# A decoder layer with a gated delta rule branch and a mixture of experts: the delta rule's 128-wide blocks merged in four staggered groups, its exponentials moved to the middle of a head, the prologue worked in halves, and the first delta rule stage placed ahead of the experts

## The reference

```
xn = layernorm(x)
out = x + delta_branch(xn) + ffn_branch(xn)

delta_branch: qkvz = xn @ W_qkvz ; ba = xn @ W_ba        # 16 key heads, 2 value heads each
  q, k, v = silu(causal_conv4(q, k, v)) ; z = gate
  beta = sigmoid(b) ; g = -exp(A_log) * softplus(a + dt_bias) ; g = cumsum(g) in a chunk of 64
  decay = tril(exp(g_i - g_j)) ; M = -tril(k_beta k^T * decay, -1)
  T = (I - M)^-1                                        # solve_triangular, per chunk
  then a scan over chunks: o = (q e^g) S + (q k^T * decay) v' ; S = S e^g_last + k'^T v'
  out = (rmsnorm(o * silu(z)) * norm_weight) @ W_out

ffn_branch: x1 = rmsnorm(xn) ; causal attention, 16 heads of 128 ; hid = xn + attn
  x2 = rmsnorm(hid) ; top 4 of 16 experts (gated, width 176) + shared expert (width 352)
  return hid + routed + shared
```

## Time and profile before

| what | value |
|---|---|
| median of 3 runs | 1630.26 us (1629.26 to 1636.0) |
| profiled execution | 1629.19 us, its span 1627.4 us |
| PE busy | 1534.4 us, 94% of the span |
| DVE busy | 1111.6 us, 68% |
| ACT busy | 784.7 us, 48% |
| POOL busy | 438.4 us, 27% |
| steady head | about 59.2 us, 14 of them |

### The profile page before, as it was taken

One profiled execution on the slowest core, in us unless ns is written; L12 is line 12 of the kernel. 1 busy time (PEld: TensorE's weight loads), 2 busy tenths in 40 slices (PEclk: granted clock), 3 DMA queues, 4 the chain that ended last, 5 costly groups with the idle time before them and its releaser, 6 DMA issues.

```text
span 1627.4 us, 29153 instructions
## 1 busy us (share of the span) xinstructions
PE 1534.4 (94%) x10922; PEld 1081.3 (66%) x10922; DVE 1111.6 (68%) x2442; ACT 784.7 (48%) x1692; POOL 438.4 (27%) x277
## 2 busy tenths in 40 slices
PE   4999999999978995699999999999999999999987
PEld 3666666766656773376677677667668668667756
DVE  4544445465362333769889889988988988888875
ACT  3444345343413433445646645646555565564641
POOL 0000000003031005226335344444532531532410
PEclk8999999999998997889999999999999999999999
DMA  3234333223323323323234144143233223323201
GB/s 97 82 116 143 131 115 104 62 70 117 87 99 108 107 85 119 90 63 82 60 99 91 46 103 103 42 100 98 60 72 82 64 65 84 69 57 88 59 11 33
DMA packets 225051, 136.88 MB, mean 84 GB/s; under 512 B 160976, under 2 KB 196304, under 8 KB 224912
## 3 DMA queue, kind: packets, MB, share of 16 engines
q1 hardware_dynamic: 221840, 126.62, 28.6%
q0 software_dynamic: 3072, 8.39, 1.6%
HBM read 94.85 MB, written 35.91 MB: 80 GB/s over the span
## 4 chain that ended last, share of the span: by engine, by line
PE 80%; issue 10%; DVE 5%; ACT 2%; POOL 1%; DMA 1%; POOLq 1%; SPq 0%; ACTq 0%; DVEq 0%
PE ps L912 7%; PE ps L811 7%; PE ps L505 6%; PE ps L830 6%; PE ps L609 4%; PE ps L530 4%; PE ps L631 3%; PE ps L520 3%; PE ps L749 3%; PE ps L851 3%; PE ps L882 3%; PE ps L759 3%; PE ps L861 2%; PE ps L881 2%; PE ps L838 2%
## 5 line engine op out<-in xcount | busy, mean ns | idle before, releaser
L1279 ACT ACTIVATE vs<-ps 128x256 f32<-128x256 f32 x128 | 49.1, 383 | 258.0 <-PE ps L851 253.7
L2027 POOL TENSOR_TENSOR qg<-qT,Ebc 128x1024 f32<-128x1024 f32 x32 | 74.9, 2360 | 357.2 <-PE ps L882 357.2
L1704 DVE SCALAR_TENSOR_TENSOR cv<-ps,cw,cv 128x1022 f32<-128x1022 f32 (+2 forms) x96 | 122.6, 1279 | 28.0 <-ACT cv L1226 24.2
L912 PE MATMUL ps<-wout,xT 128*128 128x256 f32 x512 | 128.8, 396 | 2.2 <-DVE total L1814 2.2
L811 PE MATMUL ps<-xnT,gv 128*128 128x512 f32 x256 | 120.4, 614 | 10.6 <-DVE cv L1704 10.1
L1487 DVE TENSOR_TENSOR ps<-ps,causal_neg 128x128 f32<-128x128 f32 x128 | 37.4, 292 | 131.8 <-PE ps L530 131.8
L1715 DVE SCALAR_TENSOR_TENSOR cv<-ps,cw,cv 128x1022 f32<-128x1022 f32 (+2 forms) x96 | 122.6, 1277 | 5.5 <-ACT cv L1258 3.1
L1814 DVE SCALAR_TENSOR_TENSOR total<-ps,rr,total 128x256 f32<-128x256 f32 x256 | 119.0, 481 | 9.8 <-POOL rr L2033 3.0
L830 PE MATMUL ps<-xnT,gz 128*128 128x512 f32 x256 | 122.8, 604 | 2.6 <-DVE MT L1748 2.4
L505 PE MATMUL ps<-xrT,wqk 128*128 128x512 f32 x256 | 119.5, 601 | 3.6 <-ACT we L1116 2.8
L1157 ACT ACTIVATE we<-ps,bias 128x128 f32<-128x128 f32 (+3 forms) x128 | 65.7, 525 | 106.0 <-DVE bias L1491 106.0
(11 more groups left out here) (256 smaller groups left out, 3612.4 us busy)
## 6 DMA issues: line engine op xcount, KB each, us to landing
xs_dram<-zeros SPq DMA_DIRECT2D x16, 1024.0 KB, 6.4
dec<-grow_dram SPq DMA_DIRECT2D x32, 512.0 KB, 4.8
Ebc<-erow_dram SPq DMA_DIRECT2D x32, 512.0 KB, 5.0
wqk<-in_wqk SPq DMA_DIRECT2D x16, 512.0 KB, 3.6
xn<-xs_dram SPq DMA_DIRECT2D x47, 128.0 KB, 2.1
ys_dram<-yg SPq DMA_DIRECT2D x47, 128.0 KB, 1.9
we<-in_we SPq DMA_DIRECT2D x16, 352.0 KB
wv<-in_wv SPq DMA_DIRECT2D x16, 256.0 KB, 3.3
```

Of the source, the lines that this page charges most:

```text
L912: last = mm(ps[:, output_bank(t), r * H:(r + 1) * H], xT[:, r, t * P:(t + 1) * P], wout[:, r, :], start=True, stop=True)
L1704: ins = stt(row, pair(bank)[:, :, 0:S - k], cw[:, f, i, TAPS - 1 - k:TAPS - k], row, ALU.mult, ALU.add)
L2027: tt(qg[:, r], qT[:], Ebc[:, r], ALU.mult).then_inc(fl["g_qg"], 1)
```

## The change

What it does:

1. The halves of x have semaphores of their own, and norms, transposes and projections run half by half. Roots are powers on GpSimd in place of ScalarE's square roots, and the squares of `xn` are worked out from its variance on VectorE. ScalarE takes part in copying the transposed `xr`. The value projection of round 0 goes into round 0, the gate products, their exponentials, sums, transposes and tables into rounds 1 to 5 of attention (`GATE, CUM, ROWS = 1, 3, 4`), and `growT` is written in round 5.
2. The pass h = -2 is gone as a pass. Its steps for head 0 are put ahead: `decay_rows(0)` in round 6, its masks on GpSimd between the two scatters, its exponentials at the end of round 13, key and query projections behind the shared expert's last gate product, the convolutions among the routing's last steps on VectorE, `key_squares(0)` ahead of the first slot, `scaled_decays(0)` and `key_norms(0)` behind the addition of `hid` on GpSimd. Buffers are laid out anew for it. The loops start at h = -1.
3. The merge from 64 to 128 runs in groups of four units, `side_blocks(n, g)`: group g's product beside the diagonal alternates with group g - 1's product of 128. ScalarE makes all copies but the last, which VectorE makes.
4. In a head, ScalarE makes `decays(f, 0)` behind `gate_silu(n, 1)` and `decays(f, 1)` behind the deltas of step 3. GpSimd makes `masked_decays(f)` and `relative_decays(f)` ahead of `decayed_queries(n)`. VectorE's second value convolution is cut at its last tap, with the turned blocks between.

The diff, cut to its core:

```diff
@@ TensorE, prologue
+            for n in range(2):
+                pe.wait_ge(sm["s_xn"], 4 * n + 4)
+                turn_halves(xn, n, 2 * n)
+            pe.wait_ge(sm["s_xn"], NT + 4)
+            turn_halves(xr, 0, 4)
...
+            pe.wait_ge(sm["s_trXE"], 2)
+            project_qk(0, 0, 2)
+            pe.wait_ge(sm["s_xn"], 2 * NT)
+            pe.wait_ge(sm["s_trE"], 2)
+            turn_halves(xr, 1, 0)
+            project_qk(0, 2, 4)
...
-            project_qk(0, 0, 4)
-            project_v(0)
...
             scores(0, 0)
-            pe.wait_ge(sm["s_gate_a"], 8)
             scores(0, 1)
             for k in range(B * PAIRS):
-                if k:
-                    project_v(k)
+                project_v(k)
...
+                    if i == 0 and k == GATE:
+                        gate_products()
+                    if i == 0 and k == CUM:
+                        gate_sums()
+                    if i == 0 and k == ROWS:
+                        gate_rows()
@@ TensorE, shared expert and slots
             gate_and_up(5)
+            pe.wait_ge(sm["f_act"], 5)
+            for b in range(B):
+                project_keys(0, b)
+            pe.wait_ge(sm["f_act"], 6)
+            for b in range(B):
+                project_queries(0, b)
...
+            key_squares(0)
             turn_slot(0)
@@ TensorE, the merge
+            def side_blocks(n, g):
+
+                if g == 0:
+                    pe.wait_ge(fl["v_tt"], 2 * n + 2)
+                    pe.wait_ge(fl["a_p2"], 2 * n + 2)
+                if 0 < g:
+                    pe.wait_ge(fl["a_u3"], 4 * n + g)
+                if g == 1 and n:
                     pe.wait_ge(fl["v_add"], 8 * n - 5)
+                for i in range(4):
+                    if g < 4:
+                        u = 4 * g + i
+                        beside = mm(ps[64:P, 1 - g % 2, i * 64:(i + 1) * 64], MT[0:64, u, 64:P], T64c[0:64, u, :],
+                                    start=True, stop=True)
...
+                    if g > 0:
+                        u = 4 * (g - 1) + i
+                        block = mm(ps[0:64, 1 - g % 2, i * 64:(i + 1) * 64], U3s[64:P, u, :], PT[64:P, u, 64:P],
+                                   start=True, stop=True)
@@ TensorE, a head
                 if middle:
                     key_products(n)
                 if scan:
-                    second_of_128(h)
+                    side_blocks(h, 4)
...
                 if scan:
-                    output_products(h, 4, 7)
-                if middle:
+                    output_products(h, 4, 6)
+                if middle:
+                    side_blocks(n, 0)
+                if scan:
+                    output_products(h, 6, 7)
+                if middle:
+                    side_blocks(n, 1)
                     turn_values(n, 1)
-                    first_beside_64(n)
+                    side_blocks(n, 2)
                 if scan:
                     output_products(h, 7, NT)
                 if middle:
-                    second_beside_64_and_first_of_128(n)
+                    side_blocks(n, 3)
@@ ScalarE, a head
                 if middle:
                     gate_silu(n, 1)
+                if ahead:
+                    decays(f, 0)
                 if scan:
                     for b in range(B):
                         deltas(h, 3, b)
+                if ahead:
+                    decays(f, 1)
...
+                    side_64(n, 0)
                     silu_value(n, 1)
-                if ahead:
-                    decays(f, 0)
-                if middle:
-                    beside_64(n)
-                if ahead:
-                    decays(f, 1)
-                if middle:
-                    blocks_of_128(n)
+                if middle:
+                    side_64(n, 1)
+                    block_of_128(n, 0)
+                    side_64(n, 2)
+                    block_of_128(n, 1)
+                    side_64(n, 3)
+                    block_of_128(n, 2)
@@ VectorE, a head
                 if middle:
-                    convolve_values(n, 1)
                     turned_diagonal(n, 1)
+                    convolve_values(n, 1, 1, TAPS - 1)
                     turned_beside(n)
+                    convolve_values(n, 1, TAPS - 1, TAPS)
...
-                if middle:
-                    beside_64(n)
@@ GpSimd
+            row_scales(0)
+            send_rows(0)
+            pool.wait_ge(fl["d_k"], 16 * 2)
+            pool.wait_ge(sm["s_prob"], 8 * (ROWS + 1))
+            masked_decays(0)
+            relative_decays(0)
+            row_scales(1)
+            send_rows(1)
+            pool.wait_ge(sm["f_hid"], 4)
+            pool.tensor_tensor(total[:], total[:], hid[:], ALU.add)
+            scaled_decays(0)
+            key_norms(0)
...
-            for h in range(-2, NK):
+            for h in range(-1, NK):
                 n, f = h + 1, h + 2
                 scan, middle, ahead = h >= 0, 0 <= n < NK, f < NK
...
-                if middle:
-                    decayed_queries(n)
                 if ahead:
                     masked_decays(f)
+                    relative_decays(f)
+                if middle:
+                    decayed_queries(n)
                 if scan:
                     output_norms(h)
                 if ahead:
-                    relative_decays(f)
                     scaled_decays(f)
                     key_norms(f)
```

More of the change, by code:

```diff
@@ L30 @@
 RING = 6
+GATE, CUM, ROWS = 1, 3, 4
 TURN, LOGIT, PLACE = 9, 10, 12
@@ new lines, in _, with gate_products @@
+            pe.wait_ge(sm["s_const"], 48)
+            for n in range(2):
[3 more added lines that the diff above has]
+            turn_halves(xr, 0, 4)
+            def gate_products():
+                for t in range(NT):
+                    for k in range(HK):
+                        last = mm(ps[:, 0, t * 2 * NV:(t + 1) * 2 * NV], xnT[:, k, t * P:(t + 1) * P], wba[:, k, :],
+                                  start=(k == 0), stop=(k == HK - 1))
+                last.then_inc(sm["s_gate_mm"], 1)
@@ new lines, in gate_sums, with gate_rows @@
+            def gate_sums():
+                pe.wait_ge(sm["s_const2"], 80)
+                pe.wait_ge(sm["s_gate_v"], 4)
+                g_all = g[:].rearrange("p t v -> p (t v)")
+                mm(ps[:, 1, 0:NT * NV], cum_mask[:], g_all, start=True, stop=True).then_inc(sm["s_gate_mm"], 1)
+                mm(ps[:, 2, 0:NT * NV], chunk_ones[:], g_all, start=True, stop=True).then_inc(sm["s_gate_mm"], 1)
+            def gate_rows():
+                for t in range(NT):
+                    last = pe.transpose(ps[0:NV, t // 4, (t % 4) * P:(t % 4 + 1) * P], G[:, t, :], ident[:])
+                    if t % 4 == 3:
+                        last.then_inc(sm["s_gate_mm"], 1)
@@ new lines, in _, with turn_slot @@
+            pe.wait_ge(sm["r_rows"], 5)
+            for u in range(SHT, 2 * SHT):
+                down(u)
+            def turn_slot(s):
+                pe.wait_ge(rows_in[s % RING], 16 * (s // RING + 1))
+                if s == 0:
+                    pe.wait_ge(fl["v_ck"], 2)
+                if s >= 2:
+                    pe.wait_ge(sm["m_xE"], s - 1)
+                for k in range(HK):
+                    last = pe.transpose(ps[:, 2 + s % 2, k * P:(k + 1) * P], xs[:, s % RING, k * P:(k + 1) * P], ident[:])
+                last.then_inc(sm["m_x"], 1)
@@ L1002, in _ @@
+            section_end(pe)
+            for h in range(-1, NK):
                 n, f = h + 1, h + 2
@@ L1348, in _ @@
+            take_slot(0)
+            take_slot(1)
+            for s in range(SLOTS + 2):
+                if s < SLOTS:
+                    slot_silu(s)
+                if s + 2 < SLOTS:
+                    take_slot(s + 2)
+                if s >= 2:
+                    take_output(s - 2)
+            section_end(act)
+            for h in range(-1, NK):
                 n, f = h + 1, h + 2
```

748 lines of the change are left out of this document (373 added, 375 removed).

## The result

The changed kernel takes 1649.65 us (median of 4, 1647.62 to 1654.63), the kernel before 1630.28 us. The ratio is 1.0116, 95% interval 1.0083 to 1.015: slower by 1.2%, where 1625 us and a range up to 1643 were predicted. The profiled execution has a span of 1646.4 us, 19.0 more than before.

The account below looks back on a forecast made before the run. TensorE was taken to bound the steady heads and to wait openly elsewhere. From 1629.19 us, -14.3 (prologue), -22.1 (first stage), +33 (heads) and -1.5 (tail) gave 1624.3, with 1.07 added 1625 us; range 1591 to 1643.

Parts of the forecast that it names:

- the overlap: Steady heads: GpSimd's masks fall in VectorE's triangular solve and stall its products; 2.35 us a head, 33 in 14 heads.
- the squares: Steady heads: squares of outputs wait behind the key's Silu table load, few tenths of slack; within small terms summing to 0.
- the groups: Merge in heads: pairing small matmuls saves about 0.5 us a head; with other small terms 0, bounds -0.5 and +0.7.
- the tail: Kernel's end: the 1.49 us wait for VectorE's copy of PT goes away; -1.5 us.
- Part A: Prologue: first scores at 28.0 instead of 48.76 us, partly paid back in the rounds; -14.3 us, range -17 to -11.
- The paying back: Attention rounds: value projection returns +1.2 us; gate products, sums and G transposes +5.3.
- Part B: First delta rule stage moved ahead of the experts, into TensorE's 14.56 us wait; -22.1 us, range -27 to -15.
- The two stalls of the pass h = -1: Head 0: decayed queries, two GpSimd passes, fall on the start of the solve; about 3.1 us, bounds 0 and 4.7.
- Part C: The 14 steady heads: GpSimd's new order costs 33 us, the four groups and other small terms together 0.
- R2: Rival, slower: heads lose over 3.35 us each, five products caught, delay reaching the deltas through ScalarE; 1650 us; chance 0.13.
- R1: Rival: the overlap costs nothing in the heads; 1592 us, to 1600 with a few tenths a head; chance 0.20.
- R3: Rival: the moved first stage is not covered, or head 0's blocks return no sooner; B gives -8, 1639 us; chance 0.06.

Follow-up runs that it names:

- `ab_groups`: The first two parts of the change plus four staggered groups and the cut convolution, GpSimd order unchanged, ScalarE's exponentials late; ratio 0.9873 to the kernel before.
- `after_squares`: The changed kernel with the squares of outputs ahead of the key's Silu and its table load on ScalarE; ratio 1.0082 to the kernel before.
- the first two parts alone: The changed kernel without new engine orders, four groups and cut convolution: prologue by halves and first stage ahead of experts remain; ratio 0.9761, rerun 0.9775.
- the kernel with only the masks held: Prologue and early first stage only, with GpSimd's masks in the pass h = -1 waiting for the end of head 0's solve; ratio 0.9761.
- With the masks held: The changed kernel, but GpSimd's masks don't start before the sum of the solve's fifth row is done; ratio 1.0065 to the kernel before.

## Why the prediction was wrong

**What bounds the kernel** was read right. TensorE has no wait in the heads before, and the delays that reached it lengthened the head. The step that failed is the price of the heads, put at 33 us and measured at 55.2. Of the 24 us by which the forecast missed, 10.8 are the overlap, 7.3 the squares, 4.1 the groups and 3.0 the tail; parts A and B gave 1.3 back. A steady head of the kernel before takes 58.97 us, not the 59.2 named ahead; the differences here are from 58.97.

**Part A** held: -16.4 against -14.3, inside its range. The scores came at 25.34 instead of 28.0 because the transposes began 0.5 us sooner, the way from them to the first projection was 1.4 shorter (2.53 for 3.9) and the second transposes held the projections up 0.8 less. The clock did not do it: the first eight projection matmuls took 3.70 in place of my 5.4, but the other eight 3.60 where my sum had 1.9, so that both together are the 7.3 of the forecast. The paying back, 7.0, was put at 6.5.

**Part B** held: -22.4 and +1.1 against -23.2 and +1.1. The key squares had 0.5 us of slack where I said 0.3. The two stalls of the pass h = -1 by the decayed queries are there, 2.02 us each, but at the end of the solve and not at its start, since the masks now go ahead of them. That the shared queue is what delays the blocks was shown by sending them first, at 2.9 us; in my sum it was 1.9 (16.0 - 5.6 - 8.5).

**Part C, the overlap: right mechanism, mis-sized term.** Put at 2.35 a head, measured 3.13, so 44 us where I had 33, just above my upper bound of 43. For a start just ahead of the product of 25 I had 3.1, and four such heads measured 3.3 to 3.5 at the value projections. For a start just behind it I had 1.95, and the five heads measured 1.95 to 2.35. The three that start at 3.06 to 3.54 meet four products and measured 2.6 to 3.1. What failed is the share of the cases and the end of the range. I carried the phases of the kernel before over, with the issue 2.45 to 3.63 us ahead of the copy. In the changed kernel the delay of VectorE moves the copy too, and the issue stands 2.3 to 4.0 ahead of it, so that six of 14 heads start their masks ahead of the product of 25. Two start 1.55 behind the copy and catch the product of 16, a case that I had not walked; they lost 5.3, of which 1.7 to 1.8 by the clock. I also had the place of the wait wrong. I let the value projections wait for VectorE's convolution, or the deltas; in the changed kernel TensorE waits earlier, at L799 for the correction (26.1 us in all) and at L786 for the state (5.1), and has no wait at the value projections. The one for the convolution appears only with the masks cut into pieces.

**Part C, the squares: named and taken at zero.** I wrote that they wait behind the key's Silu table load with a few tenths of slack, and summed it up with others as 0. It measured 0.52 a head, 7.3 us, and one exchange in ScalarE's order took it back at that place.

**Part C, the groups.** Put at 0 in all with the squares, from -0.5 for the pairs. The pairing does not pay: 0.3 to 0.4 a head are lost, 4 us, of which 0.2 is the guard wait on the additions in each head. Squares and groups together, +0.81, lie above the bound of +0.7 that I gave. That the rest is the changes between widths and the last tap is not shown.

**The tail** was wrong in sign, -1.5 forecast and +1.5 measured, by two steps. TensorE's wait for the copy of PT fell from 1.49 to 1.05 and that for U3s from 0.78 to 0.46. But the value transposes of the second row came 43.0 us behind the last copy of the blocks where they came at 40.7, in all kernels with the groups and the cut convolution 1.8 further behind those of the first row than in the others. I had looked at what went away and not at what the change puts ahead of these transposes. The two even out: the first scan group behind the wait for PT starts 48.56 us behind that copy, where it started at 48.36. The other 1.3 us are the clock. Behind that wait the changed kernel runs part of the stretch at the lower level, the kernel before none of it (start and end, length, busy time of PE, PEld, DVE, ACT, POOL, granted clock, DMA share, GB/s; before, then after):

```profile
1592.01:1611.71 19.70, 17.42 (x125) 15.23 (x125) 9.78 (x28) 5.36 (x12) 0.06 (x1) 1.00 0.00 1
1609.70:1630.68 20.98, 18.72 (x124) 16.73 (x124) 9.78 (x28) 5.36 (x12) 0.96 (x1) 0.92 0.00 1
```

```profile
1609.70 2.05 PE L799 MATMUL ps<-vs,PT 128*128 128x128 f32 x8 [1.05 <-DVE PT L1925]
1611.55 1.75 PE L809 MATMUL ps<-vs,WT 128*128 128x128 f32 x8
```

The same two groups take 1.13 and 1.16 before. The clock does not go with the change: `ab_groups` and `after_squares` have 1.00 in this stretch, and the first two parts alone 0.86 with the wait of 1.49.

**The rivals.** The slower one, R2, came true by its threshold: 3.94 a head is above 3.35 (3.29 with R1 at 1592.4, as its own sum gives it). Its mechanism only in part: the passes did start early enough to catch another product, but the rest came through the squares, the groups and the clock, and not through the deltas, which have no wait in the view. I gave it 0.13 because I summed the small terms of the heads to zero. R1 is out: none of the 50 products issued under a pass of GpSimd in the changed kernel kept its usual length. R3 is out: the rows are waited for 0.52 us, and the blocks are back 16.9 us behind the experts.

Two things stay open: why a wait of about 2 us is followed by a lower clock in some heads and not in others, and why the kernel with only the masks held is 4 us longer by its ratio than its trace lets one expect.

## What to carry to other kernels

Work that is put on an engine which shares something with the bound engine's feeder has to be placed by what the feeder does at that time, not by when its input lands: here 8.5 us of GpSimd work cost 3.1 us inside the solve and nothing behind it. In a loop without slack, small terms may not be summed to zero; each of them is multiplied by the number of turns, and each deserves its own bound. And if an edit shifts a chain, the phases between its members shift with it: walk all of them, not those of the trace before.

## What the runs showed of the hardware

That a VectorE product of 25 columns takes 2.31 us under a GpSimd pass was expected; that cutting the four passes into 32 instructions brings the stall down to 0.56 us at most and makes GpSimd's own work 1.6 times as long (13.2 for 8.5 us) was not. The page "SBUF — State Buffer" of the Trainium skill, section "Who interferes with whom", says that the lock is held for the whole instruction; the trace agrees, as both the long and the cut passes show.

Behind a wait of 3.40 us in an otherwise busy stretch TensorE's mean clock was 0.61 and 0.62 for the next 4.4 and 4.5 us, in both heads that had it. With the masks held, a wait of 2.19 and one of 1.78 were followed by 0.64 and 0.66 over 5 us, and with the orders alone on the kernel before four waits of 2.19 and one of 1.92 lost as much. Waits of 2.18 and 2.19 in three heads of the changed kernel, of 2.20 in one and 1.73 or 1.74 in eleven of the held one, and of 2.07 in one of the orders alone, were followed by no lower clock. So in a loop bound by TensorE a wait can cost more than its length, here about 1.7 us more, and its length alone does not tell whether it will.

The four block transfers of head 0 took 2.70 to 5.57 us to issue on the SP queue in the ten traces in which they stand right behind Ebc, 2.31 and 2.40 in the two in which they go ahead of it, and 1.97 in the kernel before, where Ebc is issued 16 us ahead of them.
